# Attention on one core: output halves, a q projection and x transposes in other steps, the big tile's product ahead of row 5's transposes

## The chip, the cores and the metric

The kernel runs on one core of a Trainium2 chip. The metric is the device time of one execution in microseconds. Below, PE is TensorE (PEld its weight loads), DVE VectorE, ACT ScalarE, POOL GpSimd and SP SyncE, the names that the profile uses.

## The reference

```python
# x: (4, 1024, 256), 16 heads of 128, 4 kv heads, causal
x = x + layernorm(attention(layernorm(x)))      # q, k with rope; softmax(q k^T / sqrt(128)) v; Wo
x = x + layernorm(moe(layernorm(x)))            # 64 experts, top 6 of 4 groups, shared expert
```

Everything is float32. The change lies in attention alone.

## The kernel before

Attention goes through 16 groups (4 batches by 4 kv heads, 4 query heads each). A group has four macros, m = 0 to 3. A macro takes two query tiles of 128 tokens, the big one (tile 7 - m, with 8 - m blocks of keys) and the small one (tile m, with m + 1 blocks), and works off eight rows: row 0 to 3 are the four heads of the big tile, row 4 to 7 those of the small tile. One step s serves a row; e = s mod 8 is its place in the macro, so there are 512 steps and a few at the end.

In step s every engine has its part, and every engine's queue is in order:
- PE: scores of row s+1 (line 331, with the mask in line 330), then the side units of the table BEFORE, then the transposes of row s-1 (line 341, one chunk of up to four blocks per PSUM buffer t_ps, two buffers), then the side units of the table AFTER (lines 398 to 406).
- DVE: the row maximum of row s+1 (line 457), its part of the BEFORE units, the low parts of row s-1's transposed probabilities (line 470), its part of the AFTER units, then a stage of a layer norm in the steps that have one (lines 521 to 532).
- ACT: its part of the BEFORE units, the high parts of row s-1's transposed probabilities (line 594), the exponential of row s+1 (line 583), its part of the AFTER units, then the rounding of a q or k whose unit ran two steps before (line 564 or 568).
- POOL: for each q or k unit the low part three steps later (line 693) and the rope, four operations, one step later (lines 677 to 682), then weight splits and the norm's apply stages. It asks only in which step a q or k unit ran.

Float32 matrix products are made of three passes with a high and a low part, hence "high" and "low" everywhere. A chunk of transposes waits until DVE has made the low part of the chunk two before. Scores of row r wait for the exponential of row r-2.

The side units are: q_0, q_1, the two halves of the next macro's q projection (line 290); k or v, here next_kv, of the next group (lines 300 and 311); next_x, four transposes of the next batch's normalized x (line 277), only in groups 2, 6 and 10; av_0 and av_1, the two halves of the product of the big tile with v (line 356), and av_small, the small tile's in one; out_0, out_1, out_2, out_3, the output projections (line 368), the first two of the previous macro's big tile and the last two of its small tile, two heads each. All of them but the av units write the one PSUM tile misc_ps. `begin_misc` lets a unit wait until the unit before it in the order MISC_ORDER has been read out: after q or k that is ACT's copy into raw (line 555), after xt and v DVE's low part (lines 447 and 453), and after an output the second addition into y by DVE, in add_output (line 501), of which there are two, one behind the other.

```python
BEFORE = {0: ('out_0',), 1: ('out_1', 'av_small'), 2: ('q_0',), 3: ('q_1',), 5: ('out_3',), 6: ('av_0',), 7: ('next_x',)}
AFTER = {3: ('out_2',), 6: ('av_1', 'next_kv')}
```

Layer norms of y, of x1 and of the next x run beside in fixed steps of each batch of 128 steps (from step 8, 25 and 44), a stage per step: nine on DVE, then the applies on POOL.

Of the kernel before, what the change touches and what calls it, by code (L numbers as in the profile page):

```python
# [64 lines left out]
    return 0 if p % 2 == 0 else part_blocks(p - 1)  # L65


BEFORE = {0: ('out_0',), 1: ('out_1', 'av_small'), 2: ('q_0',), 3: ('q_1',), 5: ('out_3',), 6: ('av_0',), 7: ('next_x',)}
AFTER = {3: ('out_2',), 6: ('av_1', 'next_kv')}


def side_units(table, s):
    if s < 0:
        return []
    macro, e = divmod(s, 8)
    g, m = divmod(macro, MACROS_PER_GROUP)
    out = []
    for name in table.get(e, ()):
        kind, part = name.split("_")
        if kind == "q" and macro + 1 < MACROS:  # L80
            out.append(("q", macro + 1, int(part)))
        elif kind == "out" and macro >= 1:
            out.append(("out", 2 * macro - 2 + int(part) // 2, int(part) % 2))
        elif kind == "av" and part == "small" and macro >= 1:
            out.append(("av", 2 * macro - 1, 2))
        elif kind == "av" and part != "small" and macro < MACROS:
            out.append(("av", 2 * macro, int(part)))
        elif kind == "next" and part == "kv" and g + 1 < GROUPS:
            out.append(("k" if m < 2 else "v", g + 1, m % 2))
        elif kind == "next" and part == "x" and macro < MACROS and g % KV_HEADS == 2 and g // KV_HEADS + 1 < B:  # L90
            out.append(("xt", g // KV_HEADS + 1, m))
    return out


def before_transposes(s):
    return side_units(BEFORE, s)


def after_transposes(s):
    return side_units(AFTER, s)  # L100

# [1371 lines left out]
```

## Time and profile before

| what | value |
|---|---|
| three runs | 2349.37 us median (2347.67 to 2354.0) |
| the profiled execution | 2355.82 us, its span 2354.0 us |
| PE busy | 1963.0 us, 83% of the span |
| DVE busy | 1407.9 us, 60% |
| POOL busy | 1389.1 us, 59% |
| ACT busy | 1097.3 us, 47% |

The span is from the first instruction to the last; the busy time is the union of an engine's instructions in it. Attention fills the span up to about 1824 us; the expert part and the last norm follow. In a timeline, instructions of one line that follow one another are merged into one row with their count, and a matmul's row reads longer than its share of the engine, since matmuls overlap: the distance of two starts tells what the first one takes.

### The profile page before, as it was taken

The page shows a single profiled execution, that of the slowest core. Times are in us where ns is not written, and L with a number is a line of the kernel's source. Part 1 is how long each engine was busy: PE and PEld are TensorE (multiplying, and loading weights), DVE is VectorE, ACT ScalarE, POOL GpSimd, SP SyncE. Part 2 cuts the span into 40 slices and gives each one's busy share as a digit, 9 for nine tenths or more (in the row PEclk, how much of TensorE's full clock was granted, in tenths as well). Part 3 has the DMA queues.
Part 4 walks back from the last instruction along what each step waited for, and adds up shares of the span by engine and source line. Part 5 has one row for each costly group of instructions (what it writes and reads, how often), then busy time and mean ns, then how long its engine had stood idle before and what let it go on. Part 6 is the DMA issues. An engine that isn't in the chain of part 4 may idle for free. (4 is left out here: it accounts for less than half of the span.)

```text
span 2354.0 us, 36240 instructions
## 1 busy us (share of the span) xinstructions
PE 1963.0 (83%) x12915; PEld 1656.1 (70%) x12915; DVE 1407.9 (60%) x3003; ACT 1097.3 (47%) x2467; POOL 1389.1 (59%) x1064
## 2 busy tenths in 40 slices
PE   3899999998899999998999999999998077466520
PEld 2788888887778888887888887788887055254320
DVE  1467766667676666776766667766666278610008
ACT  1556565665555665555565655555655011021100
POOL 6666675857677666677775857686652400135542
PEclk9999999999999999999999999999999577656655
DMA  4001000000020000002000000020000212245444
GB/s 165 15 10 32 10 15 10 15 23 1 10 86 23 10 14 10 14 10 86 10 14 10 15 10 14 10 68 19 1 2 1 77 59 63 81 136 134 104 129 169
DMA packets 75627, 99.21 MB, mean 42 GB/s; under 512 B 9480, under 2 KB 68632, under 8 KB 73928
## 3 DMA queue, kind: packets, MB, share of 16 engines
q1 hardware_dynamic: 69544, 85.64, 11.6%
q0 software_dynamic: 5920, 11.44, 2.3%
q8 instruction: 98, 1.61, 0.3%
q14 instruction: 65, 0.53, 0.1%
HBM read 71.67 MB, written 25.39 MB: 41 GB/s over the span
## 5 line engine op out<-in xcount | busy, mean ns | idle before, releaser
L331 PE MATMUL s_ps<-kT,q 128*128 128x512 f32 (+3 forms) x2304 | 597.6, 377 | 27.6 <-POOL q L693 18.5
L470 DVE TENSOR_TENSOR pT<-t_ps,pT 128x512 fp32r<-128x512 f32 (+3 forms) x768 | 401.6, 551 | 336.6 <-ACT pT L594 334.7
L331 PEld LDWEIGHTS s_ps<-kT,q 128*128 128x128 f32 x2304 | 409.0, 195 | 71.0 <-issue 17.6
L356 PE MATMUL av_ps<-pT,v 128*128 128x512 f32 x1728 | 439.1, 400 | 0.0
L680 POOL TENSOR_TENSOR rope<-raw,sinT 64x512 f32<-64x512 f32 x320 | 411.6, 1286 | 24.6
L457 DVE TENSOR_REDUCE neg_max<-s_ps 128x1 f32<-128x640 f32 (+7 forms) x512 | 384.9, 752 | 58.6 <-PE s_ps L331 52.8
L583 ACT ACTIVATE probs<-s_ps,neg_max 128x640 f32<-128x640 f32 (+7 forms) x512 | 381.6, 745 | 77.4 <-DVE neg_max L457 75.8
L594 ACT ACTIVATE pT<-t_ps 128x512 fp32r<-128x512 f32 (+3 forms) x768 | 348.6, 490 | 145.0 <-PE t_ps L341 139.4
L341 PE MATMUL t_ps<-ident,probs 128*128 128x128 f32 x2304 | 342.7, 276 | 22.2 <-ACT probs L583 13.4
L356 PEld LDWEIGHTS av_ps<-pT,v 128*128 128x128 f32 x1728 | 317.2, 191 | 60.5
L677 POOL TENSOR_TENSOR cosed<-raw,cosT 128x512 f32<-128x512 f32 x160 | 206.4, 1290 | 203.4 <-ACT raw L555 194.8
L341 PEld LDWEIGHTS t_ps<-ident,probs 128*128 128x128 f32 x2304 | 266.7, 141 | 55.2 <-ACT probs L583 18.6
L368 PE MATMUL misc_ps<-w_o,avT 128*128 128x256 f32 x1536 | 240.2, 292 | 14.1 <-DVE y L501 8.9
L368 PEld LDWEIGHTS misc_ps<-w_o,avT 128*128 128x128 f32 x1536 | 205.9, 190 | 33.8 <-ACT raw L555 12.8
L501 DVE SCALAR_TENSOR_TENSOR y<-misc_ps,inv_sum,y 128x256 f32<-128x256 f32 x448 | 215.3, 481 | 10.9 <-PE misc_ps L368 3.0
L290 PE MATMUL misc_ps<-xT,w_q 128*128 128x256 f32 x1536 | 208.2, 285 | 7.9 <-ACT raw L555 7.9
L682 POOL TENSOR_TENSOR raw<-cosed,rope 128x512 f32<-128x512 f32 x160 | 205.1, 1282 | 12.5
L290 PEld LDWEIGHTS misc_ps<-xT,w_q 128*128 128x128 f32 x1536 | 198.4, 192 | 10.2 <-ACT raw L555 9.0
L564 ACT ACTIVATE q<-raw 128x512 fp32r<-128x512 f32 x128 | 80.5, 629 | 207.7 <-POOL raw L682 207.7
L693 POOL TENSOR_TENSOR q<-raw,q 128x512 fp32r<-128x512 f32 x128 | 163.1, 1288 | 1.5 <-ACT q L564 1.5
L475 DVE TENSOR_TENSOR avT<-av_ps,avT 128x512 fp32r<-128x512 f32 x128 | 88.6, 692 | 113.7 <-ACT avT L601 113.7
L697 POOL TENSOR_TENSOR w_kv<-raw_kv,w_kv 128x512 fp32r<-128x512 f32 x16 | 20.4, 1278 | 219.2 <-ACT w_kv L607 219.2
(160 smaller groups left out, 2170.6 us busy)
## 6 DMA issues: line engine op xcount, KB each, us to landing
e_w_in<-in_expert_w SPq DMA_DIRECT2D x8, 1536.0 KB, 7.5
raw_q<-in_wpack SPq DMA_DIRECT2D x32, 256.0 KB, 2.9
raw_o<-in_wpack SPq DMA_DIRECT2D x16, 512.0 KB, 3.9
f_m<-sums SPq DMA_DIRECT2D x8, 1024.0 KB, 11.5
e_w_down<-in_expert_w SPq DMA_DIRECT2D x8, 768.0 KB, 10.1
xw<-in_x SPq DMA_DIRECT2D x4, 1024.0 KB, 7.1
raw_kv<-in_wpack SPq DMA_DIRECT2D x16, 256.0 KB, 4.3
xb<-in_x SPq DMA_DIRECT2D x4, 1024.0 KB, 8.7
```

The source lines that it names most:

```text
L290: last = pe.matmul(misc_ps[:, h * 256:(h + 1) * 256], w_q[:, s, half, c, h * HD:(h + 1) * HD], pair(xT[:, b % 2, a, c], m), start=(n == 0) ...
L331: last = pe.matmul(out, q[:, macro % 2, a, h, int(big)], kT[:, g % 2, s, lo:hi], start=(n == 0), stop=(n == 2))
L341: last = pe.transpose(t_ps[n % 2][:, j * P:(j + 1) * P], probs[:, r % 3, (first + j) * P:(first + j + 1) * P], ident[:])
L356: last = pe.matmul(av_ps[:], v[:, g % 2, a, j], pT[:, s, part_slot(p) + j], start=(j == 0 and n == 0), stop=(j == blocks - 1 and n == 2))
L368: last = pe.matmul(misc_ps[:, h * HID:(h + 1) * HID], avT[:, a, 2 * half + h], w_o[:, s, 2 * half + h], start=(n == 0), stop=(n == 2))
L457: dve.reduce_max(neg_max[:, r % 16:r % 16 + 1], s_ps[:, r % 2, 0:(row_tile(r) + 1) * P], AX.X, negate=True).then_inc(max_ready, 1)
L470: dve.tensor_tensor(lo, t_ps[n % 2][:, 0:count * P].rearrange("p (j n) -> p j n", n=P), hi.bitcast(F32), ALU.subtract).then_inc(t_lo, 1)
L501: last = dve.scalar_tensor_tensor(target[:, t], src, inv, y[:, t], ALU.mult, ALU.add)
L583: act.activation(probs[:, r % 3, 0:width], s_ps[:, r % 2, 0:width], ACT.Exp, bias=neg_max[:, r % 16:r % 16 + 1], accum_out=row_sum[:, r % ...
L594: act.activation(pT[:, 0, slot + first:slot + first + count, r % 4], t_ps[n % 2][:, 0:count * P].rearrange("p (j n) -> p j n", n=P), ACT.C ...
L677: pool.tensor_tensor(shape(cosed[:]), shape(raw[:, n % 2]), table(cosT, 0, P), ALU.mult).then_inc(cos_done, 1)
L680: pool.tensor_tensor(shape(rope[64 - lo:128 - lo]), shape(raw[lo:hi, n % 2]), table(sinT, lo, hi), ALU.mult).then_inc(sin_done, 1)
```

## The change

Five side units change their place; their work is the same.

```diff
-BEFORE = {0: ('out_0',), 1: ('out_1', 'av_small'), 2: ('q_0',), 3: ('q_1',), 5: ('out_3',), 6: ('av_0',), 7: ('next_x',)}
-AFTER = {3: ('out_2',), 6: ('av_1', 'next_kv')}
+BEFORE = {0: ('out_0',), 1: ('out_1', 'av_small'), 2: ('q_0',), 4: ('next_x',), 5: ('out_3',), 6: ('av_0', 'av_1')}
+AFTER = {2: ('out_2',), 3: ('q_1',), 6: ('next_kv',)}
```

- out_2 moves from behind the transposes of step 3 to behind those of step 2.
- q_1 moves from ahead of the transposes of step 3 to behind them.
- next_x moves from step 7 to step 4, ahead of the transposes there.
- av_1 moves from behind the transposes of step 6 to ahead of them, directly behind av_0; next_kv stays behind them.

The order in which the units take misc_ps follows: out_0, out_1, q_0, out_2, q_1, next_x, out_3, next_kv, where it was out_0, out_1, q_0, q_1, out_2, out_3, next_kv, next_x.

## Rows read from the trace of the kernel before

**Rows 1.** Busy time by stretches, PE alone: us, busy (instructions), granted clock, DMA share, GB/s.
```profile
557.50:564.30 6.80, 5.51 (x19) 0.50 0.00 0
...
860.00:960.00 100.00, 99.75 (x663) 1.00 0.05 14
```

**Rows 2.** Waits of PE from 80 to 1750 us: total us, times, longest.
```profile
PE s_ps L331 <- POOL q L693: 18.1, 6, 4.9
```

**Rows 3.** Timeline of PE, group 7, m = 1: start, us, instruction.
```profile
873.59 0.95 PE L341 MATMUL t_ps<-ident,probs 128*128 128x128 f32 x7
...
874.86 1.60 PE L290 MATMUL misc_ps<-xT,w_q 128*128 128x256 f32 x12
876.29 0.92 PE L341 MATMUL t_ps<-ident,probs 128*128 128x128 f32 x7
877.14 0.98 PE L368 MATMUL misc_ps<-w_o,avT 128*128 128x256 f32 x6
877.96 0.40 PE L331 MATMUL s_ps<-kT,q 128*128 128x256 f32 x2
...
878.45 0.95 PE L341 MATMUL t_ps<-ident,probs 128*128 128x128 f32 x7
...
880.92 0.48 PE L331 MATMUL s_ps<-kT,q 128*128 128x256 f32 x2
```

**Rows 4.** Timeline of DVE, the same macro.
```profile
874.98 1.16 DVE L470 TENSOR_TENSOR pT<-t_ps,pT 128x512 fp32r<-128x512 f32 x2
...
878.68 0.99 DVE L501 SCALAR_TENSOR_TENSOR y<-misc_ps,inv_sum,y 128x256 f32<-128x256 f32 x2
```

**Rows 5.** Timeline of ACT, the same macro.
```profile
873.84 0.62 ACT L555 ACTIVATE raw<-misc_ps 128x512 f32<-128x512 f32 x1
...
879.11 0.98 ACT L594 ACTIVATE pT<-t_ps 128x512 fp32r<-128x512 f32 x2 [0.70 <-PE t_ps L341]
```

**Rows 6.** Timelines of DVE and PE at m = 0, 2 and 3, three rows each.
```profile
849.81 1.29 DVE L470 TENSOR_TENSOR pT<-t_ps,pT 128x512 fp32r<-128x512 f32 x2 [1.27 <-ACT pT L594]
...
852.88 0.33 PE L331 MATMUL s_ps<-kT,q 128*128 128x128 f32 x2
...
853.37 1.16 PE L341 MATMUL t_ps<-ident,probs 128*128 128x128 f32 x8
...
899.36 1.02 DVE L470 TENSOR_TENSOR pT<-t_ps,pT 128x512 fp32r<-128x512 f32 x2 [1.26 <-ACT pT L594]
...
902.44 0.52 PE L331 MATMUL s_ps<-kT,q 128*128 128x384 f32 x2
...
903.10 0.82 PE L341 MATMUL t_ps<-ident,probs 128*128 128x128 f32 x6
...
925.23 0.89 DVE L470 TENSOR_TENSOR pT<-t_ps,pT 128x512 fp32r<-128x512 f32 x2 [1.36 <-ACT pT L594]
...
928.40 0.63 PE L331 MATMUL s_ps<-kT,q 128*128 128x512 f32 x2
...
929.23 0.71 PE L341 MATMUL t_ps<-ident,probs 128*128 128x128 f32 x5
```

**Rows 7.** Timelines of POOL and PE at the end of the macro of rows 3.
```profile
880.05 1.29 POOL L677 TENSOR_TENSOR cosed<-raw,cosT 128x512 f32<-128x512 f32 x1
...
885.40 2.54 POOL L693 TENSOR_TENSOR q<-raw,q 128x512 fp32r<-128x512 f32 x2
...
887.89 1.07 PE L331 MATMUL s_ps<-kT,q 128*128 128x512 f32 x5
```

**Rows 8.** Timelines at a norm step, group 4, from m = 1 to m = 2.
```profile
550.91 1.23 DVE L803 TENSOR_TENSOR newton<-rstd 128x8 f32<-128x8 f32 x1
...
550.84 1.29 POOL L677 TENSOR_TENSOR cosed<-raw,cosT 128x512 f32<-128x512 f32 x1 [2.14 <-ACT raw L555]
...
555.80 1.20 PE L331 MATMUL s_ps<-kT,q 128*128 128x512 f32 x5 [2.46 <-ACT probs L583]
```

**Rows 9.** Timeline of PE at next_x, group 6, m = 2.
```profile
809.08 0.63 PE L277 MATMUL misc_ps<-ident,xw 128*128 128x128 f32 x4 [0.39 <-DVE v L453]
```

## The prediction

> **What bounds the kernel now.** The reading begins with the busy time by stretches: in a stretch of attention without norm work TensorE is busy 99.75 of 100 us at full clock [rows 1]. So attention (some 1750 of the 2354 us) is bound by the order in which TensorE's queue can be worked off, and the reader should look for the small waits in it. The list of TensorE's waits shows few that are long; the largest sum, 18.1 us in six waits of up to 4.9, is scores that wait for the POOL operation that finishes a new q [rows 2]. Short waits, below what that list attributes, show only in the timeline as start-to-start distances, so the working below goes by these. I take one big tile far from all norm work (group 7, m = 1) on TensorE [rows 3], VectorE [rows 4] and ScalarE [rows 5], and the same places of m = 0, 2 and 3 [rows 6]. "Row 1" to "row 5" are rows of that macro, T(1) the transposes of row 1, S(5) the scores of row 5.
>
> **Parts of the change.** Nothing is added or removed: the same instructions and DMAs are issued, POOL's and SP's orders are untouched (both depend on the step of a q or k unit alone, and no such unit changes its step). Four things move.
>
> *out_2 ahead of q_1.* Before, step 3 is S(4), q_1, T(2), out_2, S(5), T(3). After, it is out_2, S(4), T(2), q_1, S(5), T(3), with out_2 behind T(1). All projections share one PSUM tile. Before, out_2 followed q_1 and waited for ScalarE's copy of raw; that wait was under T(2). After, q_1 follows out_2 and must wait until VectorE has added both halves of out_2 into y. VectorE is in order, and that addition stands behind the two low parts of row 1.
> Worked for m = 1. T(1) starts at 873.59, and T(1) and S(4) together take 1.27 (to 874.86), S(4) being about 0.56 of it [rows 3]. out_2 waits for raw of q_0, which ends at 873.84 + 0.62 = 874.46 [rows 5], so it starts at 874.51 and lasts 0.82 (877.14 to 877.96), to 875.33. S(4) and T(2), of the sizes of T(1) and S(4), take the same 1.27, to 876.60 [rows 3]. VectorE ends row 1's low parts at 874.98 + 1.16 = 876.14, and the two additions take 0.99 [rows 4]: with the overlap of 0.09 that consecutive VectorE rows show, y is done at 877.04 and q_1 starts at about 877.09, a wait of 0.5. q_1 takes 1.43 (874.86 to 876.29), S(5) 0.49 (877.96 to 878.45) [rows 3]: T(3) starts at 879.01, where it started at 878.45. That is 0.56 late.
> Part of it comes back. From T(3) to S(7) took 2.47 before (878.45 to 880.92) [rows 3], because VectorE had the addition of out_2 ahead of row 3's low parts (878.68) [rows 4]. After, that addition is gone from there; what remains is ScalarE's start 0.66 behind the transposes (879.11 - 878.45) and the first half of its 0.98, some 0.6 with its overlap [rows 5], VectorE's first low part, some 0.7 of a pair's 1.16 [rows 4], and 0.3 for the hand-over and T(4): 2.28. I carry 0.56 - 0.19, about 0.38 us.
> The same sum for the others [rows 6]: m = 0: VectorE is through with row 1 at 851.10, q_1 starts at 852.05, S(5) takes 0.49, T(3) comes at 853.97 for 853.37, 0.60 late, 0.42 after the part that comes back. m = 2: 900.38, 901.33, S(5) 0.66, T(3) at 903.42 for 903.10: 0.32 late, 0.29 kept. m = 3: 926.12, 927.07, S(5) 0.83, T(3) at 929.33 for 929.23: 0.10 late, all kept. A group of four big tiles pays 0.38 + 0.42 + 0.29 + 0.10 = 1.2 us, sixteen groups 19 us; 26 if nothing comes back, and 0 at the other end if VectorE's addition should not hold q_1 up. I take 19, since every duration in it stands in a row.
> Behind q_1's wait on TensorE stand S(5) and T(3), all on the path. POOL waits for raw of q_1, which now comes at about 878.52 + 0.2 + 0.6 = 879.3; that is hidden, since POOL is still at q_0 and only takes q_1 up at 880.05 [rows 7]. S(8) waits for POOL's last part of q_0, which came at 885.40 + 1.27 and had 1.2 us to spare before S(8) at 887.89 [rows 7]; later S(8) only widens that.
>
> *The product in one piece.* T(5) moves behind av_1. The pieces sum to the same matmuls, TensorE is full there in both orders, and the next unit, k or v, covers T(5)'s eviction: 0 (if that cover were gone, 0.7 of ScalarE and 0.7 of VectorE at most). On ScalarE and VectorE the eviction of the product now stands ahead of row 5's. Both engines are free under the product; S(9), which waits for row 7's exponential, comes only behind k or v and S(8): 0. Bound: ±0.1 us per big tile.
>
> *Where the norm makes VectorE the bound.* In groups 0 mod 4, m = 1, the Newton steps follow the product's eviction at step 6 on VectorE; the scores of the next macro's third row waited 2.46 us for an exponential there, whose row maximum stood behind Newton operations such as that at 550.91, which took 1.23 us [rows 8]. With the product's eviction first, row 5's low part no longer has to be done in advance of it and the Newton steps start some 0.6 us earlier (ScalarE's exponential of row 7 no longer stands ahead of the product's eviction), possibly ahead of POOL's operation at 550.84. I take -1.3 us in each of the three batches that have it, -4 in all (0 to -8). The Trainium skill, SBUF — State Buffer, section Who interferes with whom, states that a VectorE instruction with two SBUF inputs and a POOL one that reads SBUF block each other whole, whoever starts first. The trace agrees: the operation of 1.23 us ends at 552.14, as POOL's at 552.13 does [rows 8]; by that rule alone Newton operations that end before POOL starts are not held at all, and two of them spared would make some -2 us a time.
> At spots where VectorE or POOL is the bound anyway, the 0.3 to 0.4 us are absorbed: in the six macros whose next scores wait for POOL [rows 2], and in some ten whose steps 2 to 5 lie beside norm steps on VectorE. 16 x 0.3 = 5, so -5 (0 to -7).
>
> *next_x from step 7 to 4.* It exists in groups 2, 6 and 10 alone, 12 units. Before, the four transposes took some 0.5 of the 0.63 of their row, and for m = 2 they waited 0.39 for v's low part [rows 9]. After, it waits for raw of q_1 (ScalarE 0.60 against the S(5) of 0.49 to 0.83), and out_3 waits for VectorE's low part of xT (ScalarE 0.6, VectorE 0.7, under T(3) and S(6)): 0.3 to 0.5 us each. 12 x 0.4 = 5 less some 2 saved: +3 (-2 to +6).
>
> **Sum**: 19 - 4 - 5 + 3 = +13 us. The profiled execution took 2355.82 us (span 2354.0), so it would be 2369; it stood 6.4 above the median of 2349.37, against which the forecast is 2362.4. A measurement of this kernel can tell some 0.3%, 7 us, from no change.
>
> **Rivals.**
> *A, q_1 is not held up* (faster). The place is VectorE's addition of out_2 at step 2. If it is through before T(2) ends, that is, if VectorE runs 0.5 us ahead of the sum above, then q_1 starts at once, VectorE is free of the addition later, and T(4) comes 0.2 us earlier in each of 64 tiles: -13, with -4 from the norm and +3 from next_x, -14: 2335. For it: from 876.14 to 878.68 VectorE has only a row maximum and two low parts to do [rows 4], so it isn't short of time. Against: it cannot be early, since it waits 1.26 to 1.36 us for ScalarE before row 1's low parts [rows 6]. It decides from 0.5 us on. 0.09.
> *B, absorbed* (same). The delay of 0.4 us is taken up later in the macro, at POOL's q and at the next rows' exponential, in most tiles. It would be +3 to +5: 2353. For it: waits on POOL exist; against: long ones are six in all, and the 1.2 us of slack of rows 7 is on POOL's side. 0.17.
> *C, the clock.* The granted clock is 0.50 in 557.50 to 564.30, right after TensorE had waited [rows 1, 8]. That is the half level, 1.2 GHz, and such falls cost up to half their length. If the shorter wait there spares it in three batches, 3 x 3.4 = -10: 2353; as many new ones, since TensorE now stops at q_1 as well, give 2372. The Trainium skill, TensorE: Matmul & The Clock Gate, section What's actually happening, states that the gate follows how busy the array has been; the trace agrees, and by that rule short waits spread over a macro cost nothing in clock. 0.04 for sparing them.
> *Forecast*: 0.70. The 26 us bound with nothing absorbed is in it.
> That the change does nothing isn't open: orders on three engines differ.
>
> **Numbers.** Slower by over 0.3%: the forecast, 0.70. Same: B and C, 0.21. Faster: A, 0.09. The range leaves A out and goes from B to 26 us less a little: 2350 to 2374.
>
> **What would show it.** Right: q_1 behind T(2) with a gap of 0.3 to 0.6 us, ended by VectorE's y; T(3) to S(7) shorter by 0.1 to 0.2; distance of macros in group 7 longer by 0.42, 0.38, 0.29, 0.10; the wait at 555.80 shorter. Wrong: q_1 starting right behind T(2), or equal distances of macros; then the sum's first term falls. If S(9) waits for an exponential, the one-piece product was mispriced.

## The result and the profile after

The changed kernel takes **2359.81 us** (median of 6 runs, 2358.8 to 2364.33) beside 2349.09 for the kernel before (6 runs, 2347.63 to 2354.0): a ratio of 1.0044 [1.003, 1.0057], 10.7 us slower. The forecast was 13 us slower. The sign, the first term of the sum and the place of the new wait came out as worked; the gain near the norm steps came, but from another part of the change than the prediction named, and larger. That the total came as near as it did is in part luck, as the last part of the account shows. The profiled execution took 2364.33 us. Four side units have changed their place: out_2, q_1, next_x and av_1; next_kv stands where it stood.

Two lines of the changed kernel's page, and two stretches of TensorE with the columns of [rows 1]:

```profile
span 2362.5 us, 36240 instructions
PE 1963.2 (83%) x12915; PEld 1651.2 (70%) x12915; DVE 1397.0 (59%) x3003; ACT 1110.0 (47%) x2467; POOL 1389.4 (59%) x1064
```
```profile
860.00:960.00 100.00, 99.03 (x642) 1.00 0.05 14
...
704.00:711.00 7.00, 7.00 (x31) 0.52 0.04 8
```

Every engine has the instructions that it had. TensorE and POOL are busy as long as before; VectorE is busy 10.9 us less and ScalarE 12.7 us more. Far from norm work TensorE now stands still 0.97 us in 100 instead of 0.25 [rows 1]. The list of TensorE's waits from 80 to 1830 us, with the columns of [rows 2], says at what:

```profile
PE s_ps L331 <- POOL q L693: 16.1, 8, 4.1
PE misc_ps L290 <- DVE y L501: 13.0, 50, 0.7
PE misc_ps L368 <- DVE y L501: 10.6, 10, 2.2
```

The second row is the predicted wait: q_1 (line 290) waits for VectorE's addition into y, 50 times and 13.0 us in all. The list of the kernel before has no such row.

The big tile of [rows 3], in the changed kernel (TensorE, then VectorE, then ScalarE):

```profile
882.46 0.93 PE L341 MATMUL t_ps<-ident,probs 128*128 128x128 f32 x7
883.31 0.98 PE L368 MATMUL misc_ps<-w_o,avT 128*128 128x256 f32 x6
884.13 0.40 PE L331 MATMUL s_ps<-kT,q 128*128 128x256 f32 x2
...
884.62 0.95 PE L341 MATMUL t_ps<-ident,probs 128*128 128x128 f32 x7
885.90 1.69 PE L290 MATMUL misc_ps<-xT,w_q 128*128 128x256 f32 x12 [0.33 <-DVE y L501]
887.43 0.40 PE L331 MATMUL s_ps<-kT,q 128*128 128x256 f32 x2
...
887.92 0.93 PE L341 MATMUL t_ps<-ident,probs 128*128 128x128 f32 x7
...
890.19 0.48 PE L331 MATMUL s_ps<-kT,q 128*128 128x256 f32 x2
```
```profile
883.78 1.16 DVE L470 TENSOR_TENSOR pT<-t_ps,pT 128x512 fp32r<-128x512 f32 x2 [0.30 <-ACT pT L594]
884.86 0.99 DVE L501 SCALAR_TENSOR_TENSOR y<-misc_ps,inv_sum,y 128x256 f32<-128x256 f32 x2
```
```profile
885.28 0.98 ACT L594 ACTIVATE pT<-t_ps 128x512 fp32r<-128x512 f32 x2 [0.17 <-PE t_ps L341]
```

out_2 stands behind T(1), and its additions end at 884.86 + 0.99 = 885.85. q_1 starts 0.05 later, 1.28 behind T(2). The transposes take 1.27 - 0.56 = 0.71 of that ahead of scores, by the prediction's reading of [rows 3], and 0.85 ahead of a projection (876.29 to 877.14 there). So the wait is between 0.43 and 0.57; the row attributes 0.33 to it. From T(3) to S(7) it takes 890.19 - 887.92 = 2.27, worked as 2.28, 2.47 before [rows 3].

Below, the "distance" of a macro is the time from its first score row (the scores issued at e = 0) to that of the next macro, on TensorE; the last macro's ends with the last output projection (line 368). All distances are differences of starts in timelines like these. The 64 macros by kind, against the profile of the kernel before:

| macros | changed, first profile | changed, second profile (e8) |
|---|---|---|
| 30 away from norms and next_x | +10.9 | +9.5 |
| 12 of groups 2, 6, 10 (next_x) | +8.7 | +8.4 |
| m = 1 to 3 of groups 4, 8, 12 (first norm) | -9.6 | -8.7 |
| m = 2 of groups 1, 5, 9 (a later norm) | -1.1 | -2.8 |
| m = 0, 1 of groups 5, 9, 13 (waits for POOL) | +1.5 | +1.5 |
| group 15 | +0.6 | +0.7 |
| all 64 | +11.1 | +8.6 |

In the first profile of the change m = 2 and 3 of group 5 take 31.53 and 28.02; the granted clock was 0.52 from 704 to 711 (the row above). In the second they take 29.79 and 26.57, so those 3.2 us belong to one execution and not to the change.

### The profile page after: what moved, and what is told of

Same layout as the page of the kernel before. It is cut to its first block and busy times, and to the rows that moved or that the text cites. A ratio compares the mean times of both kernels' runs of the same rounds, so it can differ in the third digit from the quotient of the medians.

```text
span 2362.5 us, 36240 instructions
## 1 busy us (share of the span) xinstructions
PE 1963.2 (83%) x12915; PEld 1651.2 (70%) x12915; DVE 1397.0 (59%) x3003; ACT 1110.0 (47%) x2467; POOL 1389.4 (59%) x1064
## 3 DMA queue, kind: packets, MB, share of 16 engines
q8 instruction: 98, 1.61, 0.3%
## 5 line engine op out<-in xcount | busy, mean ns | idle before, releaser
L331 PE MATMUL s_ps<-kT,q 128*128 128x512 f32 (+3 forms) x2304 | 593.8, 376 | 16.6 <-POOL q L693 16.1
L356 PE MATMUL av_ps<-pT,v 128*128 128x512 f32 x1728 | 419.0, 393 | 0.0
L341 PEld LDWEIGHTS t_ps<-ident,probs 128*128 128x128 f32 x2304 | 267.2, 141 | 46.2 <-issue 11.1
L290 PE MATMUL misc_ps<-xT,w_q 128*128 128x256 f32 x1536 | 214.6, 290 | 21.0 <-DVE y L501 13.0
```

Source lines behind the costliest of these rows:

```text
L290: last = pe.matmul(misc_ps[:, h * 256:(h + 1) * 256], w_q[:, s, half, c, h * HD:(h + 1) * HD], pair(xT[:, b % 2, a, c], m), start=(n == 0) ...
L331: last = pe.matmul(out, q[:, macro % 2, a, h, int(big)], kT[:, g % 2, s, lo:hi], start=(n == 0), stop=(n == 2))
L341: last = pe.transpose(t_ps[n % 2][:, j * P:(j + 1) * P], probs[:, r % 3, (first + j) * P:(first + j + 1) * P], ident[:])
L356: last = pe.matmul(av_ps[:], v[:, g % 2, a, j], pT[:, s, part_slot(p) + j], start=(j == 0 and n == 0), stop=(j == blocks - 1 and n == 2))
```

## The experiments

Edits are against the kernel before unless said otherwise. The kernel before was timed in every round: 2349.72 (25 runs) beside e1 to e4, 2349.52 (10) beside e5 to e8, 2351.89 (6) beside e9 to e11, 2351.3 (17) beside e12.

### e1: the swap of out_2 and q_1 alone

```diff
-BEFORE = {0: ('out_0',), 1: ('out_1', 'av_small'), 2: ('q_0',), 3: ('q_1',), 5: ('out_3',), 6: ('av_0',), 7: ('next_x',)}
-AFTER = {3: ('out_2',), 6: ('av_1', 'next_kv')}
+BEFORE = {0: ('out_0',), 1: ('out_1', 'av_small'), 2: ('q_0',), 5: ('out_3',), 6: ('av_0',), 7: ('next_x',)}
+AFTER = {2: ('out_2',), 3: ('q_1',), 6: ('av_1', 'next_kv')}
```

> Only out_2 and q_1 are exchanged; product and next_x stay as before. Theory 1 (the swap is the whole cost, the norm gain is the product's): macros of group 7 longer by about 0.4, 0.3, 0.3 and 0.2 us, q_1 waiting 0.2 to 0.6 us for VectorE's y in each; macro m = 2 of group 4 stays near 33.8 us; in all +14 to +18 us. Theory 2 (the norm gain comes from the swap, which takes the addition out of VectorE's way): the same in group 7, but m = 2 of group 4 falls to 30 to 31 us, in all +7 to +10 us.

Measured: 2352.98 us (10 runs), 1.0014 [1.0005, 1.0024]. Group 7 is longer by 0.43, 0.29, 0.40 and 0.22 us for m = 0 to 3: the whole steady cost of the change is the swap's. But m = 2 of groups 4, 8 and 12 falls from 33.84, 34.01, 33.38 to 30.23, 30.20, 30.87. So the gain at the norm is the swap's as well. The places are those of theory 2, but the 3.3 us in all lie below the 7 to 10 us that it gave: more comes back than either theory had.

### e2: the product in one piece alone

```diff
-BEFORE = {0: ('out_0',), 1: ('out_1', 'av_small'), 2: ('q_0',), 3: ('q_1',), 5: ('out_3',), 6: ('av_0',), 7: ('next_x',)}
-AFTER = {3: ('out_2',), 6: ('av_1', 'next_kv')}
+BEFORE = {0: ('out_0',), 1: ('out_1', 'av_small'), 2: ('q_0',), 3: ('q_1',), 5: ('out_3',), 6: ('av_0', 'av_1'), 7: ('next_x',)}
+AFTER = {3: ('out_2',), 6: ('next_kv',)}
```

> Only av_1 moves ahead of the transposes of step 6. Theory 1: group 7 within 0.05 us per macro of before, m = 2 of group 4 shorter by 2 to 3 us, in all -5 to -8 us. Theory 2: m = 2 of group 4 unchanged within 0.5 us, in all 0 to -1 us.

Measured: 2348.91 us (10 runs), 0.9994 [0.9984, 1.0004]; group 7 within 0.06 us in every macro; m = 2 of groups 4, 8, 12 takes 32.90, 32.88, 33.16. The product in one piece costs nothing, and brings 0.2 to 1.1 us at a norm, not the bulk of it. VectorE, then POOL, e2, group 4:

```profile
548.51 0.15 DVE L803 TENSOR_TENSOR newton<-rstd 128x8 f32<-128x8 f32 x1
...
549.11 1.13 DVE L806 TENSOR_TENSOR rstd<-rstd,newton 128x8 f32<-128x8 f32 x1
```
```profile
548.93 1.28 POOL L677 TENSOR_TENSOR cosed<-raw,cosT 128x512 f32<-128x512 f32 x1 [1.81 <-ACT raw L555]
```

The first Newton operation does come ahead of POOL's, as the prediction had it for this part of the change. But the fourth one, at 549.11, then meets POOL's operation and takes 1.13 us.

### e3: the change with next_x left in step 7

Against the changed kernel:

```diff
-BEFORE = {0: ('out_0',), 1: ('out_1', 'av_small'), 2: ('q_0',), 4: ('next_x',), 5: ('out_3',), 6: ('av_0', 'av_1')}
+BEFORE = {0: ('out_0',), 1: ('out_1', 'av_small'), 2: ('q_0',), 5: ('out_3',), 6: ('av_0', 'av_1'), 7: ('next_x',)}
```

> The changed kernel with next_x back in step 7. Both theories: the macros of group 6 fall from 29.30, 26.01, 26.91, 27.43 us to about 28.5, 25.05, 27.0, 27.5 us, so that next_x at step 4 is worth +1.7 us per group that has it; in all -5 us against the changed kernel, +5 to +7 against before. If next_x costs nothing by its place, it equals the changed kernel within 1 us.

Measured: 2350.67 us (10 runs), 1.0014 [1.0004, 1.0023]. A group with next_x takes 28.51, 25.20, 27.05, 27.39 here (group 6) and 29.30, 26.01, 26.91, 27.43 in the changed kernel: +0.79, +0.81, -0.14, +0.04. That is 1.5 us a group and 4.5 in three. Between the whole kernels the ratios leave some 7 us (1.0044 against 1.0014). So 4.5 us are placed in next_x's groups. The rest is not: the sums of the 64 macros of the two profiles of the changed kernel lie 8.4 and 6.0 us above this one's, in part by where half-clock stretches fell. Against the kernel before, e3 is 1 us slower by the medians and 3 by the ratio, where 5 to 7 were expected.

The changed kernel at next_x, group 6, m = 0, TensorE's timeline:

```profile
753.50 0.63 PE L277 MATMUL misc_ps<-ident,xw 128*128 128x128 f32 x4 [0.42 <-ACT raw L555]
...
755.54 0.99 PE L368 MATMUL misc_ps<-w_o,avT 128*128 128x256 f32 x6 [0.18 <-DVE xT L447]
```

Both predicted waits are there: next_x waits 0.42 for ScalarE's copy of raw, and out_3 0.18 for VectorE's low part of xT. At m = 2 and 3, with longer scores in between, they are nearly hidden.

### e4: one-piece product, and next_x behind the transposes of step 7

Against e2:

```diff
-BEFORE = {0: ('out_0',), 1: ('out_1', 'av_small'), 2: ('q_0',), 3: ('q_1',), 5: ('out_3',), 6: ('av_0', 'av_1'), 7: ('next_x',)}
-AFTER = {3: ('out_2',), 6: ('next_kv',)}
+BEFORE = {0: ('out_0',), 1: ('out_1', 'av_small'), 2: ('q_0',), 3: ('q_1',), 5: ('out_3',), 6: ('av_0', 'av_1')}
+AFTER = {3: ('out_2',), 6: ('next_kv',), 7: ('next_x',)}
```

> The product in one piece, out_2 and q_1 as before, next_x behind the transposes of step 7. Theory 1: as the product alone, with another -0.3 us for m = 2 and 3 of groups 2, 6 and 10, since 0.25 to 0.35 us of transposes then lie under the wait for v's low part: -6 to -9 us against before, ahead of both kernels. Theory 2: -1 to -3 us.

Measured: 2363.06 us (4 runs), 1.0059 [1.0042, 1.0076]; a miss, it is slower. In group 6, m = 1, 2, 3 and the macro behind it take 1.71, 1.06, 0.91 and 1.61 us more. TensorE's waits, e4:

```profile
PE misc_ps L368 <- DVE xT L447: 16.7, 12, 1.6
```

What I had overlooked: the next unit on misc_ps is out_0 of the next macro, with one score row between, and it waits for ScalarE's and VectorE's copies of xT, up to 1.6 us, 12 times.

### e5: q_1 in step 4, behind everything it waited for

Against e3:

```diff
-BEFORE = {0: ('out_0',), 1: ('out_1', 'av_small'), 2: ('q_0',), 5: ('out_3',), 6: ('av_0', 'av_1'), 7: ('next_x',)}
-AFTER = {2: ('out_2',), 3: ('q_1',), 6: ('next_kv',)}
+BEFORE = {0: ('out_0',), 1: ('out_1', 'av_small'), 2: ('q_0',), 4: ('q_1',), 5: ('out_3',), 6: ('av_0', 'av_1'), 7: ('next_x',)}
+AFTER = {2: ('out_2',), 6: ('next_kv',)}
```

> The changed kernel with next_x back in step 7 and q_1 one unit later, ahead of the transposes of step 4, so that S(5) lies between T(2) and q_1. Theory 1 (q_1's wait for VectorE's addition of out_2 is the steady cost): the wait of 0.2 to 0.6 us goes, the macros of group 7 come within 0.15 us of before (27.66, 24.55, 25.53, 26.35), while m = 2 of group 4 keeps the gain (30 to 31 us); in all -8 to -14 us against before. Rival (the distance of out_2 and q_1 doesn't matter, VectorE's total work per row does): group 7 stays 0.25 to 0.4 us per macro above before, in all +1 to +3 us against before.

Measured: 2419.65 us (4 runs), 1.0295 [1.0273, 1.0316], 70 us slower than the kernel before, where both theories had at most 3. The wait of q_1 is gone, as expected: in group 7, m = 1, T(1) to S(7) takes 7.37 us, 7.33 in the kernel before and 7.73 in the changed one. But POOL's work on a q starts a step later, since POOL asks for q's step. Timelines of TensorE and of POOL and the list of waits, e5, group 7, m = 3:

```profile
952.18 1.55 PE L331 MATMUL s_ps<-kT,q 128*128 128x512 f32 x5 [2.30 <-POOL q L693]
```
```profile
948.44 2.37 POOL L702 TENSOR_TENSOR w_q<-raw_q,w_q 128x1024 fp32r<-128x1024 f32 x1 [3.22 <-ACT w_q L613]
950.77 1.27 POOL L693 TENSOR_TENSOR q<-raw,q 128x512 fp32r<-128x512 f32 x1
```
```profile
PE s_ps L331 <- POOL q L693: 50.8, 19, 4.9
PE t_ps L341 <- DVE pT L470: 15.7, 26, 1.3
PE misc_ps L368 <- POOL w_o L706: 12.4, 4, 4.0
```

q's last part (950.77) now stands behind a weight split (948.44), for which POOL had first stood still 3.22 us until ScalarE had made its part, and the scores of the next macro's third row wait 2.30 us for it. The waits on POOL went from 16.1 to 50.8 us. The last macro of a group (m = 3) takes 30.45 us in group 7 for 26.35. Some macros got shorter: m = 0 of groups 5, 9 and 13 takes 30.9 instead of 35.7, and m = 2 of groups 4, 8 and 12 takes 29.6 to 29.7, so the gain at the norm is kept.

### e6: e5 with next_x ahead of the product

Against e5:

```diff
-BEFORE = {0: ('out_0',), 1: ('out_1', 'av_small'), 2: ('q_0',), 4: ('q_1',), 5: ('out_3',), 6: ('av_0', 'av_1'), 7: ('next_x',)}
+BEFORE = {0: ('out_0',), 1: ('out_1', 'av_small'), 2: ('q_0',), 4: ('q_1',), 5: ('out_3',), 6: ('next_x', 'av_0', 'av_1')}
```

> As the kernel with q_1 ahead of the transposes of step 4, and next_x at step 6 ahead of the product, where some 5 us of product cover its two evictions. Theory (next_x costs through the units that wait for misc_ps behind it): groups 2, 6 and 10 come within 0.45 us per macro of groups 3, 7 and 11 in every m, another -1 to -3 us in all. Rival (its cost is ScalarE's and VectorE's time, wherever it stands): no change within 1 us.

Measured: 2435.13 us (4 runs), 1.0361 [1.0343, 1.0378], a miss for both expectations. Group 6 against e5: m = 0 +1.06, m = 1 +0.90, m = 3 +4.3. next_x doesn't find a free place there either.

### e7: the change with next_x ahead of the product

Against the changed kernel:

```diff
-BEFORE = {0: ('out_0',), 1: ('out_1', 'av_small'), 2: ('q_0',), 4: ('next_x',), 5: ('out_3',), 6: ('av_0', 'av_1')}
+BEFORE = {0: ('out_0',), 1: ('out_1', 'av_small'), 2: ('q_0',), 5: ('out_3',), 6: ('next_x', 'av_0', 'av_1')}
```

> The changed kernel with next_x at step 6 ahead of the product. Theory: macros of group 6 at those of group 7 (28.05, 24.83, 25.85, 26.59) plus 0.4 to 0.5 us; in all -6 to -10 us against the changed kernel of the same call. Rival: it equals the changed kernel within 2 us.

Measured: 2363.86 us (4 runs), 1.0065 [1.0047, 1.0083]; another miss. Group 6 takes 29.66, 26.29, 27.03, 27.57, with m = 0 and 1 dearer than in the changed kernel. TensorE, e7, group 6, m = 0:

```profile
754.01 0.63 PE L277 MATMUL misc_ps<-ident,xw 128*128 128x128 f32 x4 [1.04 <-DVE y L501]
```

One row of a small tile lies between out_3 and next_x, and that is less than VectorE needs for out_3's additions.

### e8: the changed kernel again

> The changed kernel itself, on the chip of the kernels of this call, to compare them with. Both theories: macros of group 6 again 29.30, 26.01, 26.91, 27.43 us. If the two long macros of group 5 (31.53 and 28.02 us for m = 2 and 3, with the half clock from 704 us on) were the accident of one execution, they are at 29.8 and 26.6 here; if they belong to the kernel, they are long again.

Measured: 2360.51 us (7 runs), 1.0041 [1.0028, 1.0053]. The result repeats. Distances agree with the first profile within 0.05 us in all but a few macros: m = 2 of groups 4 and 12 and m = 2 and 3 of group 5, where the half clock fell otherwise, m = 0 and 1 of group 9, which trade 0.4 us, the first and the last.

### e9, e10, e11: the norms elsewhere

These ask whether what the change gets back near norm steps hangs on where the norms stand.

e9, and then e10; e11 is e10 with the tables of the changed kernel:

```diff
-Y_NORM, X1_NORM, X_NORM = 8, 25, 44
+Y_NORM, X1_NORM, X_NORM = 8, 39, 56
```
```diff
-Y_NORM, X1_NORM, X_NORM = 8, 39, 56
+Y_NORM, X1_NORM, X_NORM = 14, 39, 56
```

> The order of before; the layer norm of x1 starts at step 39 of a batch instead of 25 and that of the next x at 56 instead of 44, so that POOL's four applies of x1 lie in m = 2 of the second group instead of its m = 0, beside no k rope. Theory 3 (the long macros are norm operations of POOL and VectorE that meet in macros in which POOL is full): m = 0 of groups 5, 9 and 13 falls from 35.7 to 28 to 29 us, m = 2 of groups 1, 5, 9 from 30 to 31 to 26 to 29, m = 2 of groups 4, 8, 12 stays at 33.5 to 34; in all -20 to -30 us. Rival (the norm work costs the same wherever it stands): the macros that take it over grow by as much, in all 0 to -3 us.

Measured: 2373.35 us (4 runs), 1.0094 [1.0076, 1.0112], 21.5 us slower where both expectations had it faster or the same. m = 0 of groups 5, 9, 13 falls from 35.7 to 27.65, as hoped. But m = 0 of groups 2, 6, 10 rises from 28.1 to 38.65, and m = 2 of groups 5, 9 and 13 from 29.70, 31.25 and 25.53 to 33.3 to 33.5. Timelines of TensorE and POOL, e9, end of m = 0 of group 6:

```profile
766.37 2.26 PE L331 MATMUL s_ps<-kT,q 128*128 128x512 f32 x5 [7.62 <-POOL q L693]
```
```profile
762.58 2.42 POOL L715 TENSOR_SCALAR xw<-xw,mv,rstd 128x256 f32<-128x256 f32 x2
764.96 1.26 POOL L693 TENSOR_TENSOR q<-raw,q 128x512 fp32r<-128x512 f32 x1
```

The applies of x's norm (line 715) now stand ahead of q's last part on POOL, and the scores wait 7.62 us for it.

> As the kernel with the two norms moved, and the norm of y from step 14 instead of 8, so that its applies lie in m = 2 and 3 of a batch's first group. Theory 3: m = 2 of groups 4, 8 and 12 falls from 33.5 to 34 us to 26 to 29 as well; in all -35 to -50 us. Rival: 0 to -3 us.

Measured: 2370.5 us (4 runs), 1.0086 [1.0064, 1.0108], a miss as well. m = 2 of groups 4, 8, 12 comes down to 28.0, 28.0, 29.4, and m = 3 goes up from 26.95 to between 33.0 and 33.8. The macros that took a norm over in e9 and e10 (m = 0 of groups 2, 6 and 10, m = 2 of group 13, m = 3 of groups 4, 8 and 12) are 6.0 to 10.6 us longer than they were.

> The same three norm positions in the changed kernel. Theory 3 with theory 2 (the changed order pays 1.2 us per group everywhere, and got back about 14 us only where norm operations had met): with nothing left to get back the changed order is 19 + 4 us, less 1 to 3 for places where it is absorbed, slower than the same norm positions in the order of before, that is by +18 to +23 us. Rival (the changed order's gain at the norm steps is its own, not a matter of where they fall): +8 to +12 us, as between the two kernels themselves.

Measured: 2374.43 us (4 runs), 1.0107 [1.0081, 1.0133], that is 3.9 us above e10 by the medians and 6.6 in the profiles' attention. Both expectations (18 to 23 and 8 to 12 us) lie above that. So the changed order does not cost its full 19 us with the norms elsewhere either: it gets most of it back there too (m = 0 of groups 2, 6 and 10 at 37.65 for 38.65, m = 2 of group 5 at 33.1 for 34.55). The gain is not tied to one spot of the kernel before.

### e12: the swap only beside norms

The swapped tables of e1 in six macros, those of the kernel before in all others:

```diff
+NEAR_NORM_BEFORE = {**BEFORE, 3: ()}
+NEAR_NORM_AFTER = {**AFTER, 2: ('out_2',), 3: ('q_1',)}
+def near_norm(macro):
+    g, m = divmod(macro, MACROS_PER_GROUP)
+    b = g // KV_HEADS
+    return (g % KV_HEADS == 0 and b >= 1 and m == 1) or (g % KV_HEADS == 1 and b + 1 < B and m == 2)
```

> The order of before, with out_2 and q_1 exchanged in six macros alone: m = 1 of groups 4, 8 and 12, and m = 2 of groups 1, 5 and 9, in whose steps 2 to 5 VectorE has stages of a norm between its row work. Theory 2 (the swap costs 0.2 to 0.45 us in a macro without norm work, and gives back where VectorE is behind, since the addition no longer stands between the norm stages of steps 11 to 13 or 51 to 53): group 7 as before within 0.05 us, m = 1 of groups 4, 8, 12 at 25.1 us, the m = 2 behind them at 30 to 32 us instead of 33.4 to 34.0, m = 2 of groups 1, 5, 9 at 29.8; in all -9 to -15 us, ahead of both kernels. Rival (the gain needs the swap in all macros, as a shift of the whole schedule against the clock or the DMAs): the long macros stay, in all within 3 us of before.

Measured: 2347.92 us (12 runs) beside 2351.3, 0.9993 [0.9982, 1.0004]. Steady macros are as before. m = 2 of group 4 takes 31.35, but of groups 8 and 12 33.80 and 33.86. m = 1 of groups 4, 8 and 12 takes 25.5, not 25.1. The 9 to 15 us of theory 2 did not come: the kernel is 3.4 us faster by the medians and 1.6 by the ratio, about what the rival has. At groups 8 and 12 the gain needs the swap in other macros too. It beats neither the kernel before nor e2 by more than can be measured.

## What happens at the norm

This is where the prediction's mechanism was partly wrong, and the same places can be laid side by side. TensorE from m = 1 to m = 2 of group 4, changed kernel:

```profile
556.29 1.18 PE L331 MATMUL s_ps<-kT,q 128*128 128x512 f32 x5
...
558.46 1.19 PE L331 MATMUL s_ps<-kT,q 128*128 128x512 f32 x5
...
562.08 0.98 PE L368 MATMUL misc_ps<-w_o,avT 128*128 128x256 f32 x6 [2.18 <-DVE y L501]
...
564.86 1.17 PE L331 MATMUL s_ps<-kT,q 128*128 128x512 f32 x5
...
566.93 1.70 PE L290 MATMUL misc_ps<-xT,w_q 128*128 128x256 f32 x12 [0.66 <-DVE y L501]
```

Kernel before, those of the same places that [rows 8] doesn't have:

```profile
550.98 1.19 PE L331 MATMUL s_ps<-kT,q 128*128 128x512 f32 x5
...
558.79 1.65 PE L368 MATMUL misc_ps<-w_o,avT 128*128 128x256 f32 x6 [1.55 <-DVE y L501]
...
563.93 1.36 PE L331 MATMUL s_ps<-kT,q 128*128 128x512 f32 x5
```

The differences of starts, with S(n) the scores of row n of m = 2 and "end" the next macro's:

| group 4 unless said | S(1) to S(2) | S(2) to out_1 | out_1 to S(3) | S(3) to end | sum | half clock |
|---|---|---|---|---|---|---|
| before | 4.82 | 2.99 | 5.14 | 20.89 | 33.84 | 6.8 us |
| changed, first profile | 2.17 | 3.62 | 2.78 | 21.63 | 30.20 | none |
| changed, e8 | 2.17 | 3.62 | 4.16 | 21.81 | 31.75 | 3.4 + 3.4 |
| e1, swap alone | 2.17 | 3.64 | 2.78 | 21.64 | 30.23 | none |
| e2, product alone | 2.95 | 3.95 | 4.32 | 21.69 | 32.90 | 3.4 + 3.4 |
| e12, group 4 | 2.17 | 3.63 | 2.76 | 22.79 | 31.35 | 3.4 |
| e12, group 8 | 4.88 | 2.99 | 4.13 | 21.80 | 33.80 | 3.4 + 3.4 |
| e3 (swap and product), group 4 | 2.17 | 3.62 | 4.38 | 20.70 | 30.87 | 3.4 |
| before, group 12 | 4.82 | 2.99 | 4.87 | 20.70 | 33.38 | 6.8 us |

Two things are in it. The wait at [rows 8], 2.46 us before, is gone (-2.65); the wait of out_1 behind it grew (+0.63), a net of -2.0. Where TensorE's granted clock fell to the half level (1.2 GHz) behind these waits, the stretch from out_1 to S(3) took 3.9 to 5.1 us; without a fall, 2.8. That shortens this stretch by another 2.36 us in the first profile of the change and by 0.98 in its second. Part of it is given back behind S(3): without a fall TensorE comes early, and q_1 waits for VectorE's y (0.66 at 566.93), so that S(3) to S(4) takes 5.28 us, with a fall ahead of it 4.35 (e3). A fall of 3.4 that is spared is worth 0.67 in the sum (30.87 and 30.20). The swap's own cost doesn't show in this macro: where the clock is full from S(3) on, the last column is 20.70 with the swap (e3) and without it (before, group 12). The macro ahead, m = 1, takes 25.10 for 25.58 besides, although a steady m = 1 pays 0.28.

Why the wait went is to be seen in VectorE's and POOL's rows. VectorE and POOL, kernel before:

```profile
545.00 1.22 DVE L434 TENSOR_SCALAR var<-mv 128x8 f32<-128x8 f32 x1
...
552.38 1.14 DVE L805 TENSOR_SCALAR newton<-newton 128x8 f32<-128x8 f32 x1
```
```profile
544.90 1.30 POOL L682 TENSOR_TENSOR raw<-cosed,rope 128x512 f32<-128x512 f32 x1
```

VectorE and POOL, changed kernel:

```profile
550.33 0.16 DVE L434 TENSOR_SCALAR var<-mv 128x8 f32<-128x8 f32 x1
550.53 1.28 DVE L435 TENSOR_SCALAR rstd<-var 128x8 int32<-128x8 int32 x1
...
555.13 0.16 DVE L803 TENSOR_TENSOR newton<-rstd 128x8 f32<-128x8 f32 x1
...
555.53 0.17 DVE L805 TENSOR_SCALAR newton<-newton 128x8 f32<-128x8 f32 x1
```
```profile
550.50 1.28 POOL L682 TENSOR_TENSOR raw<-cosed,rope 128x512 f32<-128x512 f32 x1
...
555.85 1.28 POOL L677 TENSOR_TENSOR cosed<-raw,cosT 128x512 f32<-128x512 f32 x1 [1.56 <-ACT raw L555]
```

VectorE, e1 (its POOL starts the operation of line 682 at 548.88), then VectorE, e12, group 8 (its lines are numbered 12 higher):

```profile
548.63 0.20 DVE L434 TENSOR_SCALAR var<-mv 128x8 f32<-128x8 f32 x1
548.86 0.17 DVE L435 TENSOR_SCALAR rstd<-var 128x8 int32<-128x8 int32 x1
549.07 1.15 DVE L436 TENSOR_SCALAR rstd<-rstd 128x8 int32<-128x8 int32 x1
```
```profile
987.43 1.26 DVE L446 TENSOR_SCALAR var<-mv 128x8 f32<-128x8 f32 x1
988.73 1.22 DVE L447 TENSOR_SCALAR rstd<-var 128x8 int32<-128x8 int32 x1
989.98 1.21 DVE L448 TENSOR_SCALAR rstd<-rstd 128x8 int32<-128x8 int32 x1
```

One and the same small operation takes 0.16 to 0.20 us when it starts ahead of POOL's operation or while POOL is idle, and mostly 1.1 to 1.3, to the end of POOL's operation, when it starts behind; below, it is then called held. This holds in all 14 profiles: of these operations in attention (lines 434 to 436 and 803 to 806) the 2040 that start while POOL is idle take 0.15 to 0.18 us, and of the 601 that start more than 0.014 us behind the start of one of POOL's none ends before that one does.

Before, line 434 started 0.10 us behind POOL's operation and was held; changed, it starts 0.17 ahead and is not. The first operation at line 803 started 0.07 behind POOL's (550.91 and 550.84, [rows 8]) and took 1.23; changed, it starts 0.72 ahead, while POOL waits for raw, and takes 0.16.

Between step 5 of m = 1 and S(3) of m = 2 seven of these operations were held in the kernel before, four or five in the changed one and in e1, seven in groups 8 and 12 of e12 and five in its group 4, where line 434's operation starts 0.01 behind POOL's (546.21 and 546.20) and escapes; in group 8 it starts 0.05 behind (987.43 and 987.38). Each held one costs VectorE about 1 us, and here VectorE sets the pace of TensorE: from S(6) of m = 1 to S(3) of m = 2 it takes 23.6 to 23.9 us before, 18.4 to 20.0 in the changed kernel and e1, 22 to 23 in e2, with seven held as well, and 21.9 in e12's group 8. How much of each difference is held operations and how much is clock isn't told apart beyond the table.

The count of all of attention goes the same way: 39 are held in the kernel before and in e2, 31 in the changed kernel, 30 in e1. But holding is not the whole of what comes back: e10 and e11 have 48 each, and the changed order gets most of its cost back there too. No run took POOL's operations out of VectorE's way, so the share of holding isn't shown by an experiment.

The Trainium skill, SBUF — State Buffer, section Who interferes with whom, states that VectorE and POOL share a pair of ports under an exclusive lock, which a VectorE instruction with two SBUF inputs takes, and also `tensor_scalar` where it runs in a mode that uses both ports. The trace agrees for both kinds: line 803 has two inputs, lines 434, 435, 436 and 805 are `tensor_scalar` with one tensor input, and all are held alike (1.23 and 1.14 to 1.28 us). In which mode the latter ran no trace shows.

## Why the prediction was right or wrong

**The swap, steady.** Right in sign, mechanism and size. The prediction's terms were 0.42, 0.38, 0.29 and 0.10 us for m = 0 to 3; group 7 shows +0.39, +0.28, +0.32 and +0.24, or 1.23 us a group for 1.2. The single terms are off by -0.03, -0.10, +0.03 and +0.14, which nearly cancel. The 0.10 was mis-sized. For m = 3 the sum took q_1 as 1.43 us long, from a place where it stood behind scores; behind transposes it takes 1.53 to the next unit (885.90 to 887.43). That is 0.1 of the 0.14. For m = 1 the same 0.1 is there too, T(3) came 0.60 late (887.92 - 882.46 = 5.46 for 4.86), and 0.32 came back by the end of the macro, 0.20 of it up to S(7). The bound "26 if nothing comes back" adds up to 25 (16 times 0.56 + 0.60 + 0.32 + 0.10).

**The product in one piece.** Right: 0 was predicted, e2 measured 0.9994 [0.9984, 1.0004]. S(9) waits for no exponential.

**The norm.** Here a step failed. "-1.3 us in each of three batches" was right in sign, and its second half, Newton steps ahead of POOL's operation at 550.84, is what the trace shows. Its cause was not: the prediction named the product's eviction standing first on VectorE, and e1, without it, has the whole gain. e2, with it alone, has 0.2 to 1.1 us: the first Newton operation gets ahead of POOL's there too (548.51 and 548.93), but others are held in its place, seven as before. What moves VectorE's norm steps so that fewer are held is the swap. The size was short too: m = 1 to 3 of groups 4, 8 and 12 give 8.7 us net (e8; 9.6 in the first profile), where the prediction had 4, and 8 as the most. Had these nine macros also paid the swap's steady cost, some 2.5 us, what came back would be 11 in all, or 3.7 a batch, of which the clock has part.

**Absorption.** -5 was predicted, in macros beside norm steps and where POOL is late. m = 2 of groups 1, 5 and 9 gave 2.8 us net instead of paying 1.0. m = 0 of group 5 stayed at 35.7, bound by POOL, and group 15 paid 0.7 instead of 1.2. With the above, the swap's 19.7 (16 groups of 1.23) comes down to 4.4 in e8's 64 macros without next_x's 4.2. So 15 us came back where the prediction had 9.

**next_x.** +3 predicted, 4.2 to 4.5 measured within its groups (some 7 between the whole kernels, of which the rest is not placed). Both waits were named, and 0.3 to 0.5 us for each fits the 0.42 and 0.18 at m = 0, and the 5 us of 12 x 0.4 fit the 4.5. The 2 us taken off for a saving were mis-sized: at m = 2 it was 0.14 a unit, in three units.

**The sum.** Part by part e8's profile has 19.7 - 15.3 + 4.2 = 8.6 us, the first profile 11.1; the medians of whole runs say 10.7. So by e8 the norm and absorption terms gave back 6 us too little and the next_x term was some 1 too small; the sum overestimated attention by 2 to 4 us. That 13 lies so near 10.7 is thus in part luck. The 2 us between e8's macros and the medians are not settled. The tail of a profiled run varies more than that: behind attention it took 530.4 us in the profile of before, 522 to 531 in the others.

**Rival A**, q_1 not held up, is false: the wait is there 50 times. **Rival B**, absorbed in most tiles, is false where it was meant to hold, in steady macros, and true near the norms. **Rival C**, the clock, had a true half: falls of 6.8 us behind the norm's wait became 3.4, twice 3.4 or none. Falls stand elsewhere as well, and they differ between two executions of one kernel. Over attention the half level held 47.8 us before, and 30.7 in both profiles of the changed kernel (sums of the stretches). The kernel is slower nevertheless.

## What to carry to other kernels

When two units that share a buffer are swapped, price the new neighbour by the full chain that frees the buffer for each of them. A copy by an engine that is early (ScalarE, 0.6 us) and an addition by one that is late and in order (VectorE, behind another row's work) are different prices for the same wait. Then ask which engine takes up the result of what was moved. e5 removed the 0.5 us wait and lost 70 us, because a step's delay put POOL's work behind a weight split that itself waited for ScalarE.

Where two engines hold each other up, small shifts change how many operations are caught. Look for one duration that comes in two sizes, 0.17 and 1.2 us here, and expect gains there to be unstable: they come with one order and not with a nearly equal one, as groups 4 and 8 of e12 show.

## What the runs showed of the hardware beyond expectation

- The hold by POOL falls on 128x8 `tensor_scalar` operations with a single tensor input as on those with two (line 434: 0.16 or 1.22 us), and who starts first decides within some 0.05 us (0.10 and 0.05 us behind: held; 0.17 and 0.02 ahead and 0.01 behind: free).
- The clock's falls behind waits of 2 to 3 us at the norm differ between executions of one kernel and between batches of one execution (m = 2 of groups 4, 8 and 12 of the changed kernel: none, 3.4, 3.4 + 3.4 in the first profile and 3.4 + 3.4, 3.4, 3.4 in the second). One of 3.4 costs 0.7 to 1.2 us of a macro's distance, two cost 1.6: 30.20 without, 30.87 and 31.35 (e12) with one, 31.75 and 31.81 with two.
- A unit of twelve matmuls takes 1.43 us to the next unit behind scores (874.86 to 876.29, [rows 3]) and 1.53 behind transposes.
